# One gate chain for two chunks in the last mixture of an eight-stage transformer kernel

## The reference

```python
logits = jnp.einsum('bsd,ed->bse', tgt, Wr) + br          # 8 experts
top_v, top_i = jax.lax.top_k(logits, 2)
top_w = jax.nn.softmax(top_v, axis=-1)
h = relu(jnp.einsum('bsd,efd->bsef', tgt, W1) + b1)       # 128 -> 512 ... -> 128
o = jnp.einsum('bsef,edf->bsed', h, W2) + b2
tgt2 = sum over the two chosen experts of top_w * o
return _layer_norm(tgt + tgt2, gamma, beta)

x = x + 0.5 * _L3_ffn_ref(_layernorm(x), ...)
x = x + _L3_attn_ref(_layernorm(x), ...)
x = x + 0.5 * _L3_ffn_ref(_layernorm(x), ...)
```

## Time and profile before

| | |
|---|---|
| median of 3 runs | 3111.85 us (3109.7 to 3118.9) |
| the profiled execution's own time | 3112.11 us |
| its span, first to last instruction | 3110.4 us |
| mean granted TensorE clock | 0.934 of 2.4 GHz |
| busy: PE, PE weight load | 2657.2, 1624.1 us |
| busy: DVE, ACT, POOL | 2226.2, 1695.8, 928.1 us |
| DMA queue issued by POOL | 8192 packets, 16.79 MB |
| sends, L2838 | x128, 131.0 us busy, 1024 ns each |

### The profile page before, as it was taken

The page is one execution under the profiler, slowest core; times in us unless marked ns, Lnnn a source line. Parts: engine busy times, 40 slices in busy tenths (PEclk is TensorE's granted clock), DMA queues, the critical chain, the costliest instruction groups (busy, mean ns, idle before and its releaser), DMA issues. The chain is left out here.

```text
span 3110.4 us, 41720 instructions
## 1 busy us (share of the span) xinstructions
PE 2657.2 (85%) x13086; PEld 1624.1 (52%) x13086; DVE 2226.2 (72%) x5317; ACT 1695.8 (55%) x2926; POOL 928.1 (30%) x1099
## 2 busy tenths in 40 slices
PE   7998888989899999878998967878888998765984
PEld 5776432333377766434655533333555776654762
DVE  5565777878466578677876678788687768776675
ACT  4443476767644444575444467675343785314862
POOL 1011234333200000121000057667245217354045
PEclk8999999999999999998999978988998999767996
DMA  5802112221012133101233333222244674004762
GB/s 144 169 11 75 39 58 73 63 68 55 30 61 87 53 104 100 42 0 48 97 93 117 114 92 95 82 83 85 69 118 154 212 234 163 15 26 161 240 225 94
DMA packets 142211, 299.22 MB, mean 96 GB/s; under 512 B 23420, under 2 KB 35772, under 8 KB 134184
## 3 DMA queue, kind: packets, MB, share of 16 engines
q1 hardware_dynamic: 132216, 276.88, 28.9%
q0 software_dynamic: 8192, 16.79, 1.8%
q10 hardware_dynamic: 1584, 2.88, 0.3%
HBM read 245.96 MB, written 70.94 MB: 102 GB/s over the span
## 5 line engine op out<-in xcount | busy, mean ns | idle before, releaser
L482 POOL TENSOR_TENSOR norm_rstd<-norm_rstd,minus_half 128x4 f32<-128x4 f32 (+1 forms) x136 | 167.3, 1230 | 1101.5 <-DVE norm_rstd L469 1090.6
L1055 DVE TENSOR_REDUCE gate_scratch<-banks 128x2 f32<-128x1024 f32 (+2 forms) x320 | 344.8, 1113 | 92.6 <-PE banks L300 64.3
L1215 ACT ACTIVATE main_tiles<-banks 128x512 f32<-128x512 f32 (+1 forms) x608 | 314.8, 581 | 130.7 <-PE banks L1196 88.7
L309 PE MATMUL banks<-main_tiles_r,ffn_weights 128*128 128x512 f32 x560 | 229.1, 409 | 10.3 <-DVE main_tiles_r L750 6.0
L2853 POOL DMA_INDIRECT main_tiles<-sorted_rows_d,token_rows x128 | 139.8, 1092 | 291.3 <-DMA sorted_rows_d<-mamba_tiles 226.0
L311 PE MATMUL banks<-main_tiles_r,ffn_weights 128*128 128x512 f32 x560 | 222.6, 397 | 0.0
L310 PE MATMUL banks<-main_tiles_r,ffn_weights 128*128 128x512 f32 x560 | 222.5, 397 | 0.0
L1232 POOL TENSOR_SCALAR_AFFINE_SELECT main_tiles<-main_tiles 128x128 f32<-128x128 f32 (+2 forms) x352 | 119.7, 344 | 285.8 <-ACT main_tiles L1215 280.7
L309 PE MATMUL banks<-main_tiles_r,moe_weights 128*128 128x512 f32 x380 | 179.7, 473 | 8.3 <-DVE main_tiles_r L2960 3.7
L2952 ACT ACTIVATE main_tiles_r<-banks,tile_bias 128x512 fp32r<-128x512 f32 x192 | 132.5, 690 | 90.7 <-PE banks L311 79.0
L2312 ACT ACTIVATE main_tiles<-banks 128x512 f32<-128x512 f32 x144 | 84.7, 598 | 163.5 <-PE banks L311 153.3
(11 more groups left out here) (446 smaller groups left out, 7308.2 us busy)
## 6 DMA issues: line engine op xcount, KB each, us to landing
main_tiles<-gates_d SPq DMA_DIRECT2D x272, 256.0 KB, 3.2
moe_weights<-w_parts_d SPq DMA_DIRECT2D x60, 1024.0 KB, 5.1
mamba_tiles<-c_rows_d SPq DMA_DIRECT2D x92, 256.0 KB, 3.4
sorted_rows_d<-in_zero SPq DMA_DIRECT2D x6, 3328.0 KB, 44.9
mamba_tiles<-sorted_rows_d SPq DMA_DIRECT2D x60, 256.0 KB
sorted_rows_d<-mamba_tiles SPq DMA_DIRECT2D x60, 256.0 KB, 4.3
spare_nat<-c_rows_d SPq DMA_DIRECT2D x36, 256.0 KB, 3.4
found_d<-main_tiles SPq DMA_DIRECT2D x32, 256.0 KB, 2.0
```

The source lines that it names most:

```text
L309: eng.matmul(o, wh, hi, start=first, stop=False)
L482: eng.tensor_tensor(rstd[:, k, 1, 0:w], rstd[:, k, 0, 0:w], minus_half[:, 0:w], ALU.pow).then_inc(s.norm_pow)
L1055: eng.tensor_reduce(o.rearrange("p (n s) -> p s n", s=2)[:, :, j0:j0 + per], psum[:, b0:b0 + 2, 0:per * (k1 - k0)].rearrange("p s (n c) -> ...
L1215: eng.activation(weight_tile(u)[:, 0:width], psum[:, score_at[u], 0:width], ACT.Exp, scale=HD ** -0.5).then_inc(s.at_exp)
```

## The change

One chain handles two neighbouring chunks, `q` = 0 to 7 in place of 16 chunks. The grids of the chain are twice as wide (8 tiles of tokens by 8 experts: 64 elements where there were 32), and `pos_i` and `wts` are indexed by pair. The logits of a pair are two groups of 8 matmuls: the first is planned 10 us after the even chunk's norm and no longer waits for the chain before, but for bank 7; the second at the chain's own time. Marks, ranks, counts, rows, the power and weights of both chunks are one operation each. The sends of the even chunk are planned 9.5 us after the chain's start, those of the odd one 11.2 us later; both wait for the pair's rows. The norms keep their planned times. The planned times of chains and the begins of tiles are new. The readers (`pool_sent`, `pool_got`, `dve_m3_mix`) only find rows and weights through `place_of` and `weight_of`.

```diff
-    euler = at("euler", [P, TPC], F32)
+    euler = at("euler", [P, 2 * TPC], F32)
-    marks_b = at("gate_marks_bf", [P, 2, TPC + 1, E8], BF16)
-    pos_i = at("token_rows", [P, NC_, 2 * TPC], I32)
-    wts = at("token_weights", [P, NC_, 2, TPC], F32)
+    marks_b = at("gate_marks_bf", [P, 2, 2 * TPC + 1, E8], BF16)
+    pos_i = at("token_rows", [P, NC_ // 2, 2, 2 * TPC], I32)
+    wts = at("token_weights", [P, NC_ // 2, 2, 2 * TPC], F32)
...
     def grid3(k):
-        return g3_t[:, 32 * k:32 * k + 32].rearrange("p (t e) -> p t e", e=E8)
+        return g3_t[:, 64 * k:64 * k + 64].rearrange("p (t e) -> p t e", e=E8)
...
     def pe_gates3(eng):
-        for n, (when, key) in enumerate(gated3):
-            yield when
-            if n:
-                eng.wait_ge(*since("g3_step", base))
-            else:
-                eng.wait_ge(s.st_h, NS * NC_)
-            eng.wait_ge(*paired(key))
-            take_bank_7(eng, since("g3_step", base + 2))
+        for q, (logits_at, when) in enumerate(gated3):
+            first = opens(q)
+            for half in range(2):
+                key = ("m3", 2 * q + half)
+                yield logits_at if half == 0 else when
+                if q == 0 and half == 0:
+                    eng.wait_ge(s.st_h, NS * NC_)
+                eng.wait_ge(*paired(key))
+                take_bank_7(eng, since("g3_step", base + 2) if half else None)
...
             yield when + 6.4
             eng.wait_ge(*since("g3_step", base + 15))
             take_bank_7(eng, since("g3_step", base + 17))
-            eng.matmul(rank, before_b[:, :], marks[:, 0:TPC, :], start=True, stop=False)
-            for t in range(TPC - 1):
+            eng.matmul(rank, before_b[:, :], marks[:, 0:PT, :], start=True, stop=False)
+            for t in range(PT - 1):
...
     def dve_gates3(eng):
-            eng.wait_ge(*since("g3_mm", n + 1))
-            eng.tensor_tensor(lg, both[:, :, E8:2 * E8], row("br3"), ALU.add).then_inc(s.g3_step)
+            eng.wait_ge(*since("g3_mm", 2 * q + 2))
+            eng.tensor_tensor(lg, both[:, :, E8:2 * E8], row3("br3"), ALU.add).then_inc(s.g3_step)
...
-            gated3.append((gate_at[c], key))
-            sent_at.append(gate_at[c] + 9.5)
+            if c % 2 == 0:
+                gated3.append((norm_at[c] + 10.0, gate_at[c // 2]))
+            sent_at.append(gate_at[c // 2] + 9.5 + 11.2 * (c % 2))
...
     def pool_sent(eng):
-                    eng.wait_ge(*since("g3_step", gate3_base(cc) + PLACED))
+                    eng.wait_ge(*since("g3_step", gate3_base(cc // 2) + PLACED))
...
     plan_moe3(0, [m2_at[NC_] + after for after in (50.2, 59.7, 68.5, 88.5, 108.5, 127, 147, 167)],
-              [m2_at[NC_] + after for after in (60.1, 74, 85.3, 100.1, 120.1, 137, 157, 177)], m2_at[NC_] + 170.0, m2_at[NC_] + 214.0)
+              [m2_at[NC_] + after for after in (74.0, 100.1, 137.0, 177.0)], m2_at[NC_] + 172.0, m2_at[NC_] + 220.0)
...
     plan_moe3(1, [la_at[0] + after for after in (35.8, 52, 55, 61.7, 69, 71.2, 91, 93)],
-              [la_at[0] + after for after in (46, 62, 72, 82, 92, 102, 119, 129)], la_at[0] + 134.0, la_at[0] + 166.0)
+              [la_at[0] + after for after in (62.0, 74.0, 86.0, 107.0)], la_at[0] + 128.0, la_at[0] + 150.0)
```

More of the change, by code:

```diff
@@ L1634, in group_of, with opens, closes, gate3_steps @@
         return GROUPS3[group_no(cc)]
[L1636 to L1643, removed]
+    PT = 2 * TPC
+    def opens(q):
+        return group_of(2 * q).first == 2 * q
+    def closes(q):
+        return 2 * q + 2 == group_of(2 * q).first + group_of(2 * q).count
+    def gate3_steps(q):
+        return GATE3_STEPS + (TABLE_STEPS if closes(q) else 0)
@@ L1651, in pe_gates3 @@
     def pe_gates3(eng):
         base, bank = 0, psum[:, 7, :]
-        both, rank = bank[:, 256:320], bank[:, 320:352].rearrange("p (t e) -> p t e", e=E8)
-        for n, (when, key) in enumerate(gated3):
-            cc = key[1]
-            first = group_of(cc).first == cc
-            yield when
-            if n:
-                eng.wait_ge(*since("g3_step", base))
-            else:
-                eng.wait_ge(s.st_h, NS * NC_)
-            eng.wait_ge(*paired(key))
-            take_bank_7(eng, since("g3_step", base + 2))
[L1664 to L1670, removed]
+        both, rank = bank[:, 256:384], bank[:, 384:448].rearrange("p (t e) -> p t e", e=E8)
@@ new lines, in pe_gates3 @@
+        for q, (logits_at, when) in enumerate(gated3):
[7 more added lines that the diff above has]
+                take_bank_7(eng, since("g3_step", base + 2) if half else None)
+                (hi, lo), w = pair_of(key), 2 * RW["l3"]
+                for t in range(TPC):
+                    sl, o0 = slice(t * TILE, (t + 1) * TILE), 2 * E8 * (TPC * half + t)
+                    eng.matmul(both[:, o0:o0 + 2 * E8], hi[:, sl], routerr[:, w:w + 2 * E8], start=True, stop=False)
+                    z = eng.matmul(both[:, o0:o0 + E8], lo[:, sl], routerr[:, w:w + E8], start=False, stop=True)
+                z.then_inc(s.g3_mm)
+            marks = marks_b[:, q % 2, :, :]
@@ L1673, in pe_gates3 @@
             take_bank_7(eng, since("g3_step", base + 17))
-            eng.matmul(rank, before_b[:, :], marks[:, 0:TPC, :], start=True, stop=False)
-            for t in range(TPC - 1):
-                z = eng.matmul(rank[:, t + 1:TPC, :], ones_b[:, :], marks[:, t:t + 1, :].broadcast_to([P, TPC - 1 - t, E8]),
-                               start=False, stop=first and t == TPC - 2)
+            eng.matmul(rank, before_b[:, :], marks[:, 0:PT, :], start=True, stop=False)
+            for t in range(PT - 1):
+                z = eng.matmul(rank[:, t + 1:PT, :], ones_b[:, :], marks[:, t:t + 1, :].broadcast_to([P, PT - 1 - t, E8]),
+                               start=False, stop=first and t == PT - 2)
             if not first:
-                z = eng.matmul(rank, ones_b[:, :], marks[:, TPC:TPC + 1, :].broadcast_to([P, TPC, E8]), start=False, stop=True)
+                z = eng.matmul(rank, ones_b[:, :], marks[:, PT:PT + 1, :].broadcast_to([P, PT, E8]), start=False, stop=True)
             z.then_inc(s.gate_rank)
-            if closes(cc):
+            if closes(q):
                 yield when + 7.2
@@ L1742, in dve_gates3 @@
             eng.tensor_tensor(line3(5), line3(3), line3(2), ALU.subtract).then_inc(s.g3_step)
-            eng.tensor_tensor(marks[:, 0:TPC, :], one, two, ALU.add).then_inc(s.g3_step)
+            eng.tensor_tensor(marks[:, 0:PT, :], one, two, ALU.add).then_inc(s.g3_step)
             step, ranks = step + 2, ranks + 1
@@ L1746, in dve_gates3 @@
             eng.wait_ge(*since("g3_step", step))
-            counted = marks[:, 0:TPC if cc == group.first else TPC + 1, :]
+            counted = marks[:, 0:PT if opens(q) else PT + 1, :]
             with nc.allow_low_precision(reason="counts up to 32 are exact in bfloat16"):
```

76 lines of the change are left out of this document (44 added, 32 removed).

## The result

The changed kernel takes 3134.93 us, the median of 6 runs (3127.84 to 3140.77), beside 3110.77 for the kernel before (6 runs, 3106.55 to 3120.47). The ratio is **1.0071, with a 95% interval of 1.0055 to 1.0087**: slower by about 22 us. Forecast was 3119 with a range up to 3134, which this passes by a microsecond. The sign of the sum holds (+7), and its size is a third of what came.

The account below looks back on a forecast made before the run. The prediction took both passes' starts to be bound by POOL's sends of the first group's rows. Pass 0's +10 and pass 1's -3 gave +7 on the profiled 3112.11, so 3119 us, with a range of 3101 to 3134.

Parts of the forecast that it names:

- What bounds the starts: Start of both passes: each begins when POOL has sent its first group's rows, six chunks of eight sends.
- Pass 0, +10: Pass 0's start: sixteen sends wait for the chain after chunk 5; first matmul 2417.0 against 2406.45, taken as +10 us.
- the relief is eaten there: Pass 0, POOL: norm 5's power behind chunks 2 and 3's sends runs at 2367.2 against 2366.55, despite DVE and PE relief.
- Pass 1, -3: Pass 1's start: last send out 2.1 us earlier, and -1 for the first tiles, together -3 us.
- Its 3.9 us come off: Pass 1, DVE before the attention's x: chunk 8's chain goes, so 3.9 us of work leave the path.
- The wider operations give back 0.6: Pass 1, DVE: a pair's chain costs 0.6 us more for twice the elements, leaving the first send 3.3 us earlier.
- 48 x 1.45 + 7 x 1.24 - 0.3 = 78.0: Pass 1, POOL: 48 sends at 1.45 us in a row with seven powers at 1.24 take 78.0 us.
- Three orders costed at nothing: First half's logits waiting for a norm, third pair's gate power behind 23 sends, chunk 10's first send: each taken as no cost.
- The tile stages keep their pace: Tile stages of both passes: their pace was to stay the same.
- POOL pauses more when sends are bunched: Rival, chance 0.30: pass 1's 48 unbroken sends pause as pass 0's, +7.5 with pass 0's +12.5; 3132 us.
- DVE's relief wins: Rival, chance 0.20: each removed chain takes 5.1 us off; pass 0 -4.8, pass 1 -6.8, 3100 us.
- Both starts stay covered: Rival, chance 0.08: the chains halve and nothing else happens, 3112 us.

Follow-up runs that it names:

- the moved cast: Changed kernel with the cast that writes a pair's rows moved on DVE directly behind its reduce; 3126.87 us, 1.0058 times the kernel before.
- held single chains: Kernel before with its sixteen single chains, every even chunk's sends held until the odd chunk's rows; 3144.81 us, 1.0104.
- the four kernels of one group: Four kernels run on one chip, among them the changed kernel with norm 5's power ahead of four sends (1.0056).
- chunks 4, 5, 8 and 9 alone: Changed kernel with these four chunks in single chains at the kernel before's planned times, the other six pairs kept; 3116.02 us, 1.0024 times the kernel before.
- single chains in the new code: Changed code with every chunk alone in its chain and the old times; 3105.44 us, 0.9986 times the kernel before.
- earlier gates: New code with every chunk alone, chunks 10 to 13 gated at 67, 74, 80, 86 in place of 72, 82, 92, 102; 3109.74 us, 1.0002 times the kernel before.

## Why the prediction was right and wrong, step by step

**What bounds the starts: right.** Both passes begin when POOL has sent the first group; holding two chunks' sends in the kernel before brings both longer gaps (14.5 and 62.2, where the pairs have 13.5 and 55.1), and freeing them takes both away (1.3 and 49.1, before 1.3 and 48.2).

**Pass 0, +10: nearly right, by terms that offset.** The stretch from the first x to the transposes grew by 11.2 us (-1.0 + 12.2). Chunk 5's rows were to come 0.7 us earlier and came 3.3 us later against that x (144.6, before 141.3). The step that failed is "the relief is eaten there": norm 5's power was to be 0.65 us later and was 5.9 later, 3.0 of them against the stretch's first x. The power ran behind a pause of 2.89 us, in the row of sends ahead of it, which cost 1.73 us a send and not 1.67; the first of them started 1.8 us after chunk 3's rows and not 0.9. From the power to the rows the sum took 12.4 us (2367.2 to 2379.6), where 13.7 had been before; it measured 14.0, so the relief did not come there either. So more than the relief was lost. Two terms went the other way: a send cost 1.55 us and not 1.67, which is 1.9 us over sixteen, and the old slack was larger. The last send's start to the transposes shrank from 9.1 to 5.7 us, 3.4 where 1.9 was taken.

**Pass 1, -3: wrong in sign, and the heart of the miss.** From pass 0's last tile to pass 1's first transposes it was +4.3 (-1.3 - 1.3 + 6.9), and the -1 for the first tiles was +1.1. The terms:
- *"Its 3.9 us come off"* was the worst. The attention's fifth x came 1.3 us earlier, not 3.9, and even that is within the spread of the profiles: this stretch takes 119.4 to 123.2 us where chunk 8's chain is single and 116.9 to 121.2 where it is paired. DVE had no gap at the row that was read the earlier trace rows, but the attention has other stretches where PE decides, as in the rows of DVE above that wait for PE. Which of them held the x back is not shown.
- *"The wider operations give back 0.6"* was exact as work: 3.92 us of one chunk's chain became 4.52 for a pair. But the chain became 2.2 us longer (15.0 against 12.8), by the order on DVE. With the cast moved it took 11.0. Together with the relief, the first send came 0.9 us later against the stage's start, not 3.3 earlier.
- *"48 x 1.45 + 7 x 1.24 - 0.3 = 78.0"* came out as 80.1 with other parts: sends 48 x 1.41, 1.9 us less than taken; three gate powers at 1.87, 1.9 us more; a wait of 1.8 us for marks, which the sum had closed; the 0.3 is in the prices.
- *The idle time that closes up pays for the sends* was nearly right: the row with eight more sends is 3.3 us longer than before (80.1 against 76.8). With the chains left single the idle time stays (8.73 us) and the gap is 62.2.

The Trainium skill (VectorE: DVE Perf Modes, The TRN2 errata — SBUF-src ops pay a fixed extra latency per instruction) gave the prediction a rival price of 1.3 us saved per pair. The trace has 2 x 3.92 - 4.52 = 3.3 us of busy time saved, so on the work the rows were right and the figure of that table too low; the same section says of a larger copy that this row of the table under-predicts it. That the fifth x also moved by 1.3 us is no support for it, as that is a matter of what bounds the attention.

**Three orders costed at nothing.** The logits' freed wait: right, single chains with it are not slower (0.9986). The third pair's gate power: DVE did stand 3.76 us for it, but at 2812, 39 us before the group's last send, and PE's wait at pass 1's start ends with the row load, not with DVE:

```profile
2812.49 0.17 DVE L1779 TENSOR_SCALAR gate_scratch<-gate_scratch 128x8 f32<-128x8 f32 x1 [3.76 <-POOL gate_scratch L1704]
```

Chunk 10's first send: it never stood, and the prediction had read its place wrong. `pool_sent` is one generator and gives the sends chunk by chunk, so this send stands behind all eight of chunk 9's, whatever their planned times, and no send of chunk 9 can be queued behind it. What stood was the gate power ahead of it, and the prediction had not asked what is queued behind that.

**The tiles' stage: not forecast.** "The tile stages keep their pace" failed by +4.1 in pass 0 in these two profiles. The four kernels whose pass 0 has the kernel before's chains and sends range from 217.4 to 220.9 us, so some 2 us either way is what one profile shows without a change; all kernels range from 217.4 to 223.8. In the changed kernel the fifth tile took 9.8 us (6.9 before), with PE standing 1.77 us for DVE. No experiment pins this term.

**The rivals.** *POOL pauses more when sends are bunched* had the right result, 3132, by a wrong reason: in the rows that it priced a send fell to 1.41 and 1.55 us. Its second form, a stop in POOL's queue at the next pair, is near to what happened in small, at the gate power and not at a send (1.8 us); it took up the moved cast's gain (4.3). *DVE's relief wins* fell: held single chains have 1.0104 and pairs 1.0071, so halving the chains, with the logits' freed order in it, is worth some 10 us, and the sends cost three times that. *Both starts stay covered* fell with pass 0's 12.01 us.

That slower came out was in part luck: it had a chance of 0.44, of which 0.30 was for dearer sends, and those did not come.

What stays open: whether the two passes cost more together than each alone (1.0071 against 1.0049), the third tile of 9.3 to 11.5 us in the four kernels of one group, where the 7 us with chunks 4, 5, 8 and 9 alone lie, and where single chains in the new code gain their 4 us.

## What to carry to other kernels

Merging two short chains halves their instructions but makes the first half's output wait for the second's input; count what the output feeds, and where it feeds an in-order queue that was idle at that time, that idle time can't be used for it any more. Before taking an engine's saved work off the path, list what stands in order behind the instruction that ends the chain, since here a cast behind another chunk's statistics (3.9 us) and a power behind sends (4.4 us at the start of pass 0) each cost more than the 3.3 us of work that a pair saves. An order repaired in one queue can move the wait to the next one (here from the cast to the gate power), so read the gap at the end, not only the event that was moved. And read the stage ahead too: with earlier gates the gap shrank by 9.6 us and the attention grew by 8.2.

## What the runs showed of the hardware that was not expected

- Powers on POOL grow with their size: 1.04 us for 128x4, 1.67 us for 128x8. Twice the elements cost 60% more, where a DVE operation on 64 elements took 216 ns and one on 32 took 183.
- In a long unbroken row of indirect sends the pauses are regular and short. In pass 1 of the changed kernel, between 2798 and 2809, seven sends follow each other at 0.30 us and the next waits 1.86. POOL's timeline:

```profile
2795.28 0.96 POOL L2857 DMA_INDIRECT sorted_rows_d<-mamba_tiles,token_rows  x1 [0.30 <-issue]
2798.10 0.97 POOL L2857 DMA_INDIRECT sorted_rows_d<-mamba_tiles,token_rows  x1 [1.86 <-issue]
...
2805.70 0.96 POOL L2857 DMA_INDIRECT sorted_rows_d<-mamba_tiles,token_rows  x1 [0.30 <-issue]
2808.53 0.97 POOL L2857 DMA_INDIRECT sorted_rows_d<-mamba_tiles,token_rows  x1 [1.86 <-issue]
```

  The longer pause of the kernel before (5.29 us in the earlier trace rows) is not seen in that pass with eight pairs.
- The spread of one kernel's runs goes with the mean granted clock: 23 runs of the kernel before reach from 3099.75 us at a mean of 0.941 to 3117.33 at 0.932. One profile of a kernel therefore says little of a few microseconds over long stretches. A gap between two events of which one waits for the other can be steadier: 48.1 to 48.2 us in three kernels, 1.3 in six. But it is not always so, as pass 0's gap was 11.7 and 13.4 in two kernels whose pass 0 is the same.
